# A decoder layer on one core: key masks as a GpSimd select, Silu in two rounds, the last batch in halves, new orders on every engine

## The chip, the core and the metric
One core of a Trainium2 chip runs the whole kernel as one program. Its engines are TensorE (PE, with the weight loads shown as PEld), VectorE (DVE), ScalarE (ACT), GpSimd (POOL) and SyncE (SP, which issues most DMAs). Each works through its own list in order; semaphores join them. The metric is the time of one execution in microseconds of the device.

## What is computed
One pre-norm decoder layer over x of (8, 128, 256), with softmax cut to what matters:

```python
x = x + attn(layernorm(x))     # 16 query heads, 4 key heads of width 16, rotary positions, causal
x = x + xattn(layernorm(x))    # scores = x @ ctx.T / 16, masked per batch, softmax, @ ctx
x = x + ffn(layernorm(x))
# attn: scores = einsum('bhgnd,bhsd->bhns', q, k) / 4, so a group's four query heads are summed;
#   then a causal softmax, @ v, @ Wo + bo
# ffn: x, w_gate_up, h and w_down each go through int8 and back, one scale per row
#   gate, up = split(xq @ w1q.T); h = silu(gate) * up; out = hq @ w2q.T     # inner width 704
```

## The kernel before
Everything is tiled by batch: 128 tokens are the 128 partitions, and there are eight batches, j = 0 to 7. Nothing loops at run time; `decoder_layer` writes one list of instructions per engine, and the list at the end of each engine's block (`keep_warm(30); mean_w_first(); ...`) is the order, written out by hand. Steps of different batches are interleaved in it, so that batch 5 may be in self attention while batch 3 is in cross attention. A step waits for the semaphores of its inputs (`done`), for a ring of two or three buffers (`free`), or for a PSUM bank that the batch before still occupies (`bank_free`, `bank_r_free`).

Start (loads and weights). DMAs: SP issues w_first (Wq, Wk, Wv), x_second, wo, x, xT, three parts of w1, ctxT, w2, ctx, in this order; ScalarE issues x_zero, x_first (x of batch 0 with the rotary table and the biases) and the mask. `keep_warm(n)` runs n products of zeros, bf16, 256 columns, that nothing uses. `mean_w_first` and `centre_w_first` take the mean off the projection weights. `bias_wo` (L271) builds the output weight with its bias, and VectorE sums and centres it (`sum_wo`, `mean_wo`, `centre_wo`, L744 to L752). VectorE also sums and rotates the biases (`sum_bias`, `rope_bias`, `rope_bias_sum`, L728 to L740). `mean_ctx` (L281) gives the mean over features of each context token: per batch and feature half one fp32 product with ctxT as weights and a single moving column.

Self attention of batch j. `project` (L295) gives q, k, v; VectorE's `rotate` (L781), GpSimd's `rotate_c` (L1007) and VectorE's `rotate_sum` (L791) apply the rotary table and the bias; `transpose_qk` (L303), ScalarE's `evacuate_qk` (L546). `mask_scores` (L314) writes the causal mask to PSUM by bf16 products of an identity with the mask, `scores` (L319) adds the scores, `max_scores` (L799) takes the row maximum, which is put into a spare row of q, transposed (`transpose_q_max`, L325) and copied (`evacuate_q_max`, L552). Then the scores are made again, transposed, keys on the partitions: `mask_other_keys` and `score_keys` write the transposed causal mask `causal_T` (L330) and add the products (L343). `exp_self` (L557) gives the probabilities p_self_T, `weigh_values` (L355, L358) their product with v and their sum, `invert_sums` (L804) and `normalise_y` (L808) the mean, `project_out` (L363) and `residual_1` (L814) x1.

Cross attention: `transpose_x1`, `cross_scores` (L379), `max_cross`, `bias_cross`, `exp_cross` (L573, Exp), `transpose_cross_p`, `readout` (L390), `residual_2` (L832). `centre_ctx` on GpSimd takes the mean off the context, from what mean_ctx gave.

FFN: x is quantised (`amax_x`, `quantise_x`) and transposed (`transpose_x_int`); `gate_product` (8 instructions of 352 columns) and `up_product` (4), both L447; `silu_gate` (L645, Silu, on both halves of 352 columns), `widen_gate` (L1029, GpSimd), `hidden` (L901), `amax_h` (L906), `scale_h`, `invert_h` (L915), `quantise_h` (L650), `transpose_h` (L474), `evacuate_h` (L638), `down` (L486), `scale_down` (L920), `add_residual` (L1056, the last on VectorE, L927), the store. All Exp calls come before the first Silu; ScalarE loads the tables of a function group by an instruction of its own. `transpose_gate`, `transpose_up`, `spread_up_scale` and `transpose_w2` bring the quantised weights into place between the batches.

## Time and profile before

| | us |
|---|---|
| median of three runs (111.39 to 113.15) | 111.41 |
| profiled execution, whole | 111.01 |
| its span, first to last instruction | 109.2 |
| PE busy | 96.1 |
| DVE, ACT, POOL busy | 75.5, 64.7, 60.2 |

The table's busy times are those of one profiled execution. Matmuls are pipelined, so a busy TensorE is not one at its peak: how many instructions start in a stretch, and at which granted clock, tells more. The time of a run is some 2 us longer than the span, for what lies around the instructions.

### The profile page before, as it was taken

Reading aid. Unit: us, or ns where it says so; the run is one execution under the profiler, and the core shown is the slowest. Engines: PE = TensorE matmul, PEld = TensorE weight load, DVE = VectorE, ACT = ScalarE, POOL = GpSimd, SP = SyncE. Lnnn points to the kernel's source line nnn. Section 1 sums busy time; section 2 is a strip of 40 time slices with the busy share of each in tenths; the row PEclk is TensorE's granted clock in tenths of the full one; section 3 lists DMA queues with packets and bytes.
Section 4 is the critical chain, followed back from the end, with each engine's and each line's share of the span. In section 5 each row is a group of like instructions: output and inputs, shape, how many; then the busy total and the mean of one; then the engine's idle time right before and its main releaser. Section 6 shows DMA issues by size and latency. Waiting matters only on the chain.

```text
span 109.2 us, 2451 instructions
## 1 busy us (share of the span) xinstructions
PE 96.1 (88%) x827; PEld 74.7 (68%) x827; DVE 75.5 (69%) x216; ACT 64.7 (59%) x169; POOL 60.2 (55%) x122
## 2 busy tenths in 40 slices
PE   6998396999999999999999998766799999999850
PEld 4786284799876677687688786445687888865520
DVE  5176939978669695956984846367698868889331
ACT  1300113870859748686668493889877587788620
POOL 6364402999358994135162143255888968765430
PEclk9999959985599999999999999999999999999999
DMA  2999999700000000000000000000000000111212
GB/s 53 382 331 405 417 420 388 230 0 0 0 9 0 0 0 3 6 0 0 0 6 0 0 0 0 9 0 0 0 0 0 0 0 6 51 48 48 96 54 96
DMA packets 4522, 8.35 MB, mean 76 GB/s; under 512 B 349, under 2 KB 3358, under 8 KB 4382
## 3 DMA queue, kind: packets, MB, share of 16 engines
q1 hardware_dynamic: 4206, 7.64, 19.2%
q10 hardware_dynamic: 304, 0.56, 1.4%
q8 instruction: 7, 0.11, 0.5%
q14 instruction: 5, 0.04, 0.1%
HBM read 7.15 MB, written 1.05 MB: 75 GB/s over the span
## 4 chain that ended last, share of the span: by engine, by line
PE 71%; DVE 12%; ACT 6%; DMA 4%; issue 3%; ACTq 1%; DVEq 0%
PE ps_s L447 15%; PE ps_q L295 7%; PE ps_r L281 5%; PE ps_y L486 5%; DMA mask_sb<-in_mask 4%; PE ps_s L343 3%; PE ps_y L363 3%; PE ps_r L390 3%; PE ps_s L319 3%; PE ps_x L379 3%; PE ps_x L474 3%; PE ps_q L303 2%; PE ps_y L355 2%; PE ps_s L330 2%; PE ps_s L314 2%
## 5 line engine op out<-in xcount | busy, mean ns | idle before, releaser
L1029 POOL TENSOR_TENSOR gate_up<-gate,up_row 128x704 f32<-128x704 f32 x8 | 13.6, 1700 | 3.0 <-ACT gate L645 2.9
L255 PE MATMUL ps_s<-warm 128*128 128x256 bf16 x51 | 9.4, 361 | 1.0 <-DVE warm L679 1.0
L1041 POOL TENSOR_SCALAR x_aug<-x2c 128x256 f32<-128x256 f32 x8 | 3.8, 480 | 10.5 <-DVE x2c L832 10.4
L540 ACT ACTIVATE v_pad<-ps_q,r 128x64 f32<-128x64 f32 x8 | 2.5, 314 | 11.9 <-DVE rot L781 11.9
L804 DVE RECIPROCAL y_rsum<-ps_y 128x128 f32<-128x128 f32 x8 | 7.6, 953 | 2.3 <-PE ps_y L358 2.1
L645 ACT ACTIVATE gate<-ps_s,x_scale 128x704 f32<-128x704 f32 x8 | 6.8, 847 | 3.9 <-PE ps_s L447 3.9
L901 DVE SCALAR_TENSOR_TENSOR hid<-ps_s,x_scale,gate_up 128x704 f32<-128x704 f32 x8 | 7.6, 949 | 1.7 <-PE ps_s L447 1.4
L255 PEld LDWEIGHTS ps_s<-warm 128*128 128x128 bf16 x51 | 6.5, 131 | 3.2 <-DVE warm L679 1.0
L447 PE MATMUL ps_s<-gate_hi,x_int_T 128*128 128x352 f32 x32 | 8.4, 343 | 0.0
L1007 POOL TENSOR_TENSOR rot_c<-rot,b_rope 128x128 f32<-128x128 f32 x8 | 3.6, 455 | 8.5 <-DVE rot L781 8.5
L486 PE MATMUL ps_y<-w_T,h_T 128*128 128x256 bf16 (+1 forms) x48 | 7.5, 276 | 0.6 <-DVE ffn L920 0.6
L447 PE MATMUL ps_s<-gate_lo,x_int_T 128*128 128x352 f32 x32 | 7.8, 323 | 0.0
L650 ACT ACTIVATE h_int<-hid,h_inv 128x704 int16<-128x704 f32 x8 | 7.0, 881 | 1.0 <-PE ps_x L474 0.8
L799 DVE TENSOR_REDUCE qk_rot<-ps_s 128x4 f32<-128x512 f32 x8 | 5.5, 690 | 2.7 <-PE ps_s L319 2.7
L1056 POOL TENSOR_TENSOR y_out<-ffn,x_aug 128x256 f32<-128x256 f32 x7 | 4.8, 690 | 4.4 <-DVE ffn L920 4.4
L781 DVE TENSOR_TENSOR rot<-ps_q,rope_r 128x256 f32<-128x256 f32 x8 | 3.4, 422 | 5.5 <-PE ps_q L295 5.3
L906 DVE TENSOR_REDUCE h_amax<-hid 128x1 f32<-128x704 f32 x8 | 7.0, 876 | 0.1
L920 DVE SCALAR_TENSOR_TENSOR ffn<-ps_y,h_scale,w_row 128x256 f32<-128x256 f32 x8 | 3.9, 482 | 4.5 <-PE ps_y L486 4.3
L447 PE MATMUL ps_s<-up_int,x_int_T 128*128 128x352 f32 x32 | 7.0, 339 | 0.0
L390 PE MATMUL ps_r<-ctx_aug,p_cross_T 128*128 128x257 f32 x16 | 5.2, 407 | 1.6 <-ACT x_int_T L631 0.7
L638 ACT CAST h_T<-ps_x 128x640 bf16<-128x640 int16 x8 | 5.5, 685 | 1.7 <-PE ps_x L474 1.7
L486 PEld LDWEIGHTS ps_y<-w_T,h_T 128*128 128x128 bf16 (+1 forms) x48 | 4.0, 97 | 3.4 <-issue 1.7
(165 smaller groups left out, 282.2 us busy)
## 6 DMA issues: line engine op xcount, KB each, us to landing
w_raw<-in_w SPq DMA_DIRECT2D x2, 512.0 KB, 9.5
ctxT<-in_ctxT SPq DMA_DIRECT2D x1, 1024.0 KB, 12.3
ctx_aug<-in_ctx SPq DMA_DIRECT2D x1, 1024.0 KB, 15.6
out_x<-y_out SPq DMA_DIRECT2D x8, 128.0 KB, 1.7
x_aug<-in_x SPq DMA_DIRECT2D x1, 768.0 KB, 7.4
xT<-in_xT SPq DMA_DIRECT2D x1, 768.0 KB, 8.6
w_raw<-in_w SPq DMA_DIRECT2D x1, 704.0 KB, 13.6
x_first<-in_x_first ACTq DMA_DIRECT2D x1, 416.0 KB, 5.6
```

Source lines behind the costliest of these rows:

```text
L255: nc.tensor.matmul(ps_s[:, H - 1, 0:2 * T], warm[:, 0:P], warm[:, :], start=True, stop=True)
L295: last = nc.tensor.matmul(ps_q[:, 0:6 * QK], x_feature(j, c), wqkv_c[:, c, :, :], start=c == 0, stop=c == DC - 1)
L390: nc.tensor.matmul(ps_r[:, 0:DA], p_cross_T[:, j, :], ctx_aug[:, j, :], start=True, stop=True).then_inc(s["readout_done"], 1)
L447: last = nc.tensor.matmul(ps_s[:, first + i, 0:FH], x_int_T[:, j, c, :], w[:, c, i * FH:(i + 1) * FH], start=c == 0 and w is parts[0], sto ...
L486: last = nc.tensor.matmul(ps_y[:, 0:D], h_T[j % 2][0:n, f, :], w2_T[0:n, f, :], start=f == 0, stop=f == FC - 1)
L638: nc.scalar.copy(h_T[j % 2][:, 0:FC - 1, :], src[:, 0:(FC - 1) * T].rearrange("p (f t) -> p f t", t=T))
L645: nc.scalar.activation(gate[j % 2][:, :, :], ps_s[:, 0:2, 0:FH], ACT.Silu, scale=x_scale[:, j:j + 1]).then_inc(s["gate_ready"], 1)
L650: nc.scalar.mul(h_int[j % 2][:, :], hid[j % 2][:, :, :].rearrange("p i f -> p (i f)"), h_inv[:, j:j + 1]).then_inc(s["h_int_ready"], 1)
L804: nc.vector.reciprocal(y_rsum[j % 3][:, :], ps_ys).then_inc(s["y_rsum_done"], 1)
L901: nc.vector.scalar_tensor_tensor(hid[j % 2][:, :, :], ps_s[:, 2:4, 0:FH], x_scale[:, j:j + 1], gate_up[j % 2][:, :, :], ALU.mult, ALU.mult ...
L906: nc.vector.tensor_reduce(h_amax[:, j:j + 1], hid[j % 2][:, :, :].rearrange("p i f -> p (i f)"), AX.X, ALU.max, apply_absolute_value=True) ...
L1029: nc.gpsimd.tensor_tensor(gate_up[j % 2][:, :, :], gate[j % 2][:, :, :], up_row[:, :].rearrange("p (i f) -> p i f", i=2), ALU.mult).then_i ...
```

## The change
- `causal_T` and its products go. `score_keys` starts its PSUM groups itself; after `exp_self`, GpSimd sets the probabilities of later keys to zero with a select over 128x512 (`drop_later_keys`), and `weigh_values` waits for that.
- `mean_ctx` has 60 moving columns per product instead of one, and results 61 columns apart; it stands ahead of `weigh_values(0)`. ctxT is loaded ahead of xT and w1; x_first moves to SP's queue, wo to ScalarE's.
- The bias sums and rotations move from VectorE to GpSimd (the key bias's copy to ScalarE), the centring of wo from VectorE to ScalarE.
- The warm products write to another bank and are spread differently (30, 6, 4, 11, 7, 2 for 30, 6, 10, 5).
- `silu_gate(0)` and `(1)` come before `exp_cross(6)` and `(7)`, the other Silu calls after them, so the tables change four times in place of two.
- `transpose_h` alternates between two banks. Batch 7's gate, Silu, widening (now on VectorE), hidden product, maximum, quantisation, transposes, copies and down product run in two halves.
- Every engine's list is written in a new order. Batches of the FFN start between the last attention batches.

Cut to its core; `last_transpose_h_a` and `_b`, `last_down_a` and `_b` `last_hidden`, `last_amax_h` and their like are the old steps on half the columns, and `sum_bias`, `rope_bias` and `centre_wo` the old arithmetic on another engine (five GpSimd operations for the bias):

```diff
             sp.dma_start(w_first[:, :], w_first_in).then_inc(s["w_first_loaded"], 16)
+            sp.dma_start(x_first[:, :], x_first_in).then_inc(s["x_first_loaded"], 16)
             sp.dma_start(x_second[:, :], x_second_in).then_inc(s["x_second_loaded"], 16)
-            sp.dma_start(wo_raw[:, :], wo_in).then_inc(s["wo_loaded"], 16)
             sp.dma_start(x_aug[:, 2:B, 0:D], x_in).then_inc(s["x_loaded"], 16)
+            sp.dma_start(ctxT[:, :, :, :], ctxT_in).then_inc(s["ctxT_loaded"], 16)
             sp.dma_start(xT[:, :, :, :], xT_in).then_inc(s["xT_loaded"], 16)
             for part, (first, last) in enumerate(W1_PARTS):
                 sp.dma_start(w1_raw[:, first:last, :], w1_in[:, first:last]).then_inc(s[f"w1_{part}_loaded"], 16)
-            sp.dma_start(ctxT[:, :, :, :], ctxT_in).then_inc(s["ctxT_loaded"], 16)
             sp.dma_start(w2_raw[:, :, :], w2_in).then_inc(s["w2_loaded"], 16)
...
-                    nc.tensor.matmul(ps_s[:, H - 1, 0:2 * T], warm[:, 0:P], warm[:, :], start=True, stop=True)
+                    nc.tensor.matmul(ps_r[:, 0:2 * T], warm[:, 0:P], warm[:, :], start=True, stop=True)
...
-                nc.tensor.matmul(ps_r[:, 0:B], mean_w[0:B, :], any_diag[:, :], start=True, stop=True)
+                means = ps_r[:, 0:B * CM].rearrange("p (b n) -> p b n", n=CM)
+                nc.tensor.matmul(means[:, :, 0], mean_w[0:B, :], any_diag[:, :], start=True, stop=True)
                 pe.wait_ge(s["ctxT_loaded"], 16)
                 for j in range(B):
                     for c in range(DC):
-                        last = nc.tensor.matmul(ps_r[:, B + j:B + j + 1], ctxT[:, j, c, :], mean_w[:, 0:1],
+                        last = nc.tensor.matmul(means[:, j, 1:CM], ctxT[:, j, c, :], mean_w[:, 1:CM],
                                                 start=c == 0, stop=c == DC - 1)
...
-            def mask_keys(j, heads):
-
-                for h in heads:
-                    nc.tensor.matmul(ps_s[:, h, 0:T], ident_b[:, :], causal_T[:, :], start=True, stop=False)
-
-            def mask_other_keys(j):
-                if j == 0:
-                    done(pe, "causal_T_ready", 0)
-                done(pe, "negmax_done", j)
-                mask_keys(j, range(1, H))
-
             def score_keys(j):
 
                 done(pe, "q_max_T_ready", j)
-                mask_keys(j, range(1))
                 for h in range(H):
                     nc.tensor.matmul(ps_s[:, h, 0:T], qk_T[j % 3][h * HP:(h + 1) * HP, 1, :],
-                                     q_max_T[j % 3][h * HP:(h + 1) * HP, :], start=False, stop=True).then_inc(s["keys_done"], 1)
+                                     q_max_T[j % 3][h * HP:(h + 1) * HP, :], start=True, stop=True).then_inc(s["keys_done"], 1)
...
-                done(pe, "p_T_ready", j)
+                done(pe, "p_causal_ready", j)
...
+            def last_gate(i):
+
+                if i == 0:
+                    gate_free(LAST)
+                    done(pe, "x_int_T_ready", LAST)
+                for c in range(DC):
+                    for w in (gate_hi, gate_lo):
+                        last = nc.tensor.matmul(ps_s[:, i, 0:FH], x_int_T[:, LAST, c, :], w[:, c, i * FH:(i + 1) * FH],
+                                                start=c == 0 and w is gate_hi, stop=c == DC - 1 and w is gate_lo)
+                last.then_inc(s["last_gate_done"], 1)
...
+                bank = (ps_x, ps_q)[j % 2]
...
-                bank_free(pe, "h_T_ready", j)
+                elif j == 1:
+                    done(pe, "qk_T_ready", B - 1)
+                free(pe, "h_T_ready", j, 2)
...
+            keep_warm(30); mean_w_first(); keep_warm(6); mask_scores(0); bias_wo(); keep_warm(4); project(0)
+            keep_warm(11); transpose_qk(0); scores(0); keep_warm(7); project(1); transpose_q_max(0)
+            keep_warm(2); score_keys(0); mean_ctx(None, 0); weigh_values(0); transpose_qk(1); mask_scores(1)
+            scores(1); project(2); project_out(0); transpose_q_max(1); transpose_gate(0, "valid_ready", 0)
+            score_keys(1); transpose_qk(2); transpose_x1(0); mask_scores(2); project(3); scores(2)
+            cross_scores(0); weigh_values(1); transpose_q_max(2); transpose_qk(3); score_keys(2)
+            transpose_gate(1, "gate_lo_ready", 0); project(4); mask_scores(3); project_out(1); scores(3)
+            transpose_cross_p(0); transpose_gate(2, "gate_lo_ready", 1); transpose_qk(4); weigh_values(2)
+            transpose_q_max(3); transpose_x1(1); project(5); score_keys(3); cross_scores(1); project_out(2)
+            readout(0, "gate_lo_ready", 2); mask_scores(4); transpose_qk(5); transpose_cross_p(1); scores(4)
+            transpose_x1(2); weigh_values(3); transpose_q_max(4); cross_scores(2); score_keys(4)
+            readout(1, "x2_ready", 0); project(6); mask_scores(5); project_out(3)
+            transpose_x_int(0, "x2_ready", 1); scores(5); transpose_cross_p(2); weigh_values(4)
+            readout(2, "x_int_T_ready", 0); transpose_q_max(5); transpose_x1(3); transpose_qk(6); score_keys(5)
+            cross_scores(3); project_out(4); mask_scores(6); project(7); scores(6); transpose_cross_p(3)
+            transpose_x_int(1, "x2_ready", 2); weigh_values(5); transpose_q_max(6); transpose_x1(4)
+            transpose_qk(7); score_keys(6); readout(3, "x_int_T_ready", 1); cross_scores(4); mask_scores(7)
+            spread_up_scale(0, "x2_ready", 3); scores(7); project_out(5); transpose_cross_p(4)
+            spread_up_scale(1, "up_row_ready", 0); transpose_q_max(7); transpose_x1(5); weigh_values(6)
+            readout(4, "up_row_ready", 1); score_keys(7); cross_scores(5); transpose_x_int(2, "x2_ready", 4)
+            gate_product(0); project_out(6); transpose_up(0, "x_int_T_ready", 2); transpose_cross_p(5)
+            weigh_values(7); gate_product(1); readout(5, "up_int_ready", 0); transpose_x1(6); project_out(7)
+            transpose_up(1, "x2_ready", 5); cross_scores(6); transpose_x_int(3, "up_int_ready", 1)
+            up_product(0); gate_product(2); transpose_x_int(4, "x_int_T_ready", 3); up_product(1)
+            transpose_cross_p(6); transpose_x_int(5, "x_int_T_ready", 4); transpose_x1(7)
+            readout(6, "x_int_T_ready", 5); cross_scores(7); transpose_w2(0, "x2_ready", 6); up_product(2)
+            transpose_cross_p(7); transpose_w2(1, "w2_ready", 0); gate_product(3); transpose_h(0)
+            readout(7, "w2_ready", 1); gate_product(4); transpose_h(1); up_product(3)
+            transpose_x_int(6, "x2_ready", 7); gate_product(5); down(0); up_product(4); gate_product(6)
+            up_product(5); transpose_h(2); down(1); transpose_x_int(7, "x_int_T_ready", 6); transpose_h(3)
+            up_product(6); last_gate(0); down(2); transpose_h(4); last_gate(1); down(3); up_product(7)
+            transpose_h(5); down(4); transpose_h(6); down(5); down(6); last_transpose_h_a()
+            last_transpose_h_b(); last_down_a(); last_down_b()
...
             act.dma_start(x_aug[:, 0, 0:D], x_zero_in).then_inc(s["x_zero_loaded"], 16)
-            act.dma_start(x_first[:, :], x_first_in).then_inc(s["x_first_loaded"], 16)
             act.dma_start(mask_sb[:, :], mask_in).then_inc(s["mask_loaded"], 16)
+            act.dma_start(wo_raw[:, :], wo_in).then_inc(s["wo_loaded"], 16)
...
+            copy_key_bias(); centre_wo(); scale_v(0); evacuate_qk(0); evacuate_q_max(0); scale_v(1); exp_self(0)
+            quantise_w1(0); quantise_w1(1); evacuate_qk(1); quantise_w1(2); quantise_w1(3); scale_v(2)
+            evacuate_q_max(1); square_1(0); upper_gate(0); exp_self(1); evacuate_qk(2); evacuate_x1(0)
+            quantise_w1(4); scale_v(3); quantise_w2(0); evacuate_q_max(2); evacuate_qk(3); exp_self(2)
+            upper_gate(1); exp_cross(0); quantise_w2(1); scale_v(4); evacuate_cross_p(0); upper_gate(2)
+            evacuate_qk(4); square_1(1); evacuate_q_max(3); evacuate_x1(1); scale_v(5); exp_self(3)
+            exp_cross(1); evacuate_cross_p(1); square_2(0); evacuate_x1(2); evacuate_q_max(4); square_1(2)
+            evacuate_qk(5); exp_self(4); quantise_x(0); square_2(1); exp_cross(2); evacuate_x_int(0); scale_v(6)
+            evacuate_cross_p(2); square_1(3); quantise_x(1); evacuate_q_max(5); evacuate_x1(3); evacuate_qk(6)
+            exp_self(5); square_2(2); exp_cross(3); quantise_x(2); scale_v(7); evacuate_cross_p(3); square_1(4)
+            evacuate_q_max(6); evacuate_x_int(1); evacuate_x1(4); exp_self(6); evacuate_qk(7); square_2(3)
+            exp_cross(4); evacuate_up_scale(0); evacuate_cross_p(4); evacuate_up_scale(1); evacuate_q_max(7)
+            square_1(5); evacuate_x1(5); quantise_x(3); exp_self(7); square_2(4); evacuate_x_int(2)
+            exp_cross(5); silu_gate(0); evacuate_up(0); evacuate_cross_p(5); quantise_x(4); square_1(6)
+            silu_gate(1); evacuate_x1(6); evacuate_up(1); quantise_x(5); evacuate_x_int(3); exp_cross(6)
+            evacuate_x_int(4); square_1(7); evacuate_cross_p(6); evacuate_x_int(5); evacuate_x1(7); square_2(5)
+            quantise_h(0); exp_cross(7); silu_gate(2); square_2(6); evacuate_cross_p(7); quantise_x(6)
+            silu_gate(3); quantise_h(1); evacuate_h(0); silu_gate(4); square_2(7); evacuate_x_int(6)
+            quantise_h(2); silu_gate(5); quantise_x(7); evacuate_h(1); quantise_h(3); silu_gate(6)
+            quantise_h(4); evacuate_x_int(7); evacuate_h(2); evacuate_h(3); last_silu(0); quantise_h(5)
+            last_silu(1); evacuate_h(4); quantise_h(6); evacuate_h(5); evacuate_h(6); last_quantise_h(0)
+            last_quantise_h(1); last_evacuate_h_a()
...
+            stats_1(0); aggregate_1(0, 1); sum_wq(); copy_ident(); find_valid(); centre_w_first(); stats_1(1)
+            aggregate_1(1, 2); exclude(); rotate(0); stats_1(2); rotate_sum(0); stats_1(3); stats_1(4)
+            stats_1(5); stats_1(6); max_scores(0); stats_1(7); aggregate_1(2, B); rotate(1)
+            amax_w1(0); scale_w1(0); invert_w1(0); rotate_sum(1); amax_w1(1); scale_w1(1); invert_w1(1)
+            invert_sums(0); keep_valid(); normalise_y(0); max_scores(1); rotate(2); residual_1(0); rotate_sum(2)
+            amax_w1(2); scale_w1(2); invert_w1(2); amax_w2(); scale_w2(); invert_w2(); rotate(3); max_scores(2)
+            rotate_sum(3); lower_gate(0); invert_sums(1); max_cross(0); normalise_y(1); bias_cross(0); rotate(4)
+            lower_gate(1); rotate_sum(4); residual_1(1); max_scores(3); invert_cross_sum(0); negate_ctx_mean()
+            invert_sums(2); normalise_y(2); rotate(5); lower_gate(2); max_cross(1); bias_cross(1); rotate_sum(5)
+            residual_2(0); residual_1(2); amax_x(0); max_scores(4); invert_cross_sum(1); invert_sums(3)
+            step_x(0); invert_x(0); normalise_y(3); max_cross(2); residual_2(1); bias_cross(2); amax_x(1)
+            rotate(6); residual_1(3); step_x(1); invert_x(1); max_scores(5); rotate_sum(6); invert_cross_sum(2)
+            invert_sums(4); residual_2(2); normalise_y(4); amax_x(2); max_cross(3); step_x(2); invert_x(2)
+            bias_cross(3); residual_1(4); rotate(7); max_scores(6); rotate_sum(7); invert_sums(5)
+            invert_cross_sum(3); normalise_y(5); residual_2(3); max_cross(4); bias_cross(4); amax_x(3)
+            max_scores(7); residual_1(5); invert_cross_sum(4); step_x(3); invert_x(3); residual_2(4)
+            invert_sums(6); max_cross(5); bias_cross(5); normalise_y(6); amax_x(4); step_x(4); invert_x(4)
+            invert_cross_sum(5); residual_1(6); invert_sums(7); normalise_y(7); residual_2(5); amax_x(5)
+            step_x(5); invert_x(5); residual_1(7); max_cross(6); bias_cross(6); hidden(0); amax_h(0)
+            scale_h(0); invert_h(0); invert_cross_sum(6); hidden(1); residual_2(6); max_cross(7); bias_cross(7)
+            amax_x(6); evacuate_w2(0); step_x(6); invert_x(6); amax_h(1); invert_cross_sum(7); evacuate_w2(1)
+            scale_h(1); invert_h(1); hidden(2); residual_2(7); amax_h(2); amax_x(7); scale_h(2); invert_h(2)
+            step_x(7); invert_x(7); hidden(3); amax_h(3); scale_h(3); invert_h(3); scale_down(0); hidden(4)
+            amax_h(4); scale_h(4); invert_h(4); hidden(5); scale_down(1); amax_h(5); hidden(6)
+            scale_h(5); invert_h(5); scale_down(2); amax_h(6); last_widen(0); scale_h(6); invert_h(6)
+            scale_down(3); last_hidden(0); last_widen(1); last_amax_h(0); scale_down(4); last_hidden(1)
+            last_amax_h(1); scale_down(5); last_scale_h(); scale_h(7); invert_h(7); scale_down(6)
+            last_evacuate_h_b(); scale_down(7); add_residual(7)
...
+            def drop_later_keys(j):
+
+                done(pool, "p_T_ready", j)
+                nc.gpsimd.affine_select(out=p_self_T[j % 3][:, :, :], in_=p_self_T[j % 3][:, :, :], compare_op=ALU.is_ge, fill=0.0, base=0,
+                                        pattern=[[0, H], [1, T]], channel_multiplier=-1).then_inc(s["p_causal_ready"], 1)
...
+            rstd_1(0, 1, 1); scale_rope(0); sum_bias(); rope_bias(); rotate_c(0); centre_x(0); rstd_1(1, 2, 2)
+            centre_x(1); scale_rope(1); rotate_c(1); rstd_1(2, B, 3); drop_later_keys(0); scale_rope(2)
+            centre_x(2); rescale_gate(0); scale_rope(3); rescale_gate(1); rotate_c(2); centre_x(3)
+            scale_rope(4); centre_x(4); rstd_2(0); drop_later_keys(1); rescale_gate(2); rotate_c(3); centre_x(5)
+            scale_rope(5); scale_rope(6); centre_x(6); centre_x(7); drop_later_keys(2); rotate_c(4)
+            scale_rope(7); centre_ctx(0); centre_ctx(1); rstd_2(1); rotate_c(5); drop_later_keys(3)
+            centre_ctx(2); whole_x2(0); rstd_2(2); scale_x(0); drop_later_keys(4); rotate_c(6); centre_ctx(3)
+            rstd_2(3); drop_later_keys(5); rotate_c(7); centre_ctx(4); scale_x(1); rstd_2(4); centre_ctx(5)
+            centre_ctx(6); drop_later_keys(6); centre_ctx(7); whole_x2(1); scale_x(2); rstd_2(5); scale_x(3)
+            drop_later_keys(7); whole_x2(2); widen_gate(0); scale_x(4); rstd_2(6); whole_x2(3); widen_gate(1)
+            rstd_2(7); scale_x(5); whole_x2(4); whole_x2(5); widen_gate(2); whole_x2(6); widen_gate(3)
+            scale_x(6); widen_gate(4); widen_gate(5); scale_x(7); widen_gate(6); add_residual(0); whole_x2(7)
+            add_residual(1); add_residual(2); add_residual(3); add_residual(4); add_residual(5); add_residual(6)
```

## Rows read from the trace of the kernel before
**Rows 1.** The page of before, parts 1 and 2: engines' busy time, granted clock.
```profile
PE 96.1 (88%) x827; PEld 74.7 (68%) x827; DVE 75.5 (69%) x216; ACT 64.7 (59%) x169; POOL 60.2 (55%) x122
...
PEclk9999959985599999999999999999999999999999
```

**Rows 2.** Windows: stretch, length, busy PE PEld DVE ACT POOL, PEclk, DMA.
```profile
0.00:31.35 31.35, 27.22 (x193) 22.24 (x193) 21.25 (x70) 9.65 (x23) 16.98 (x45) 0.84 0.62 229
31.35:60.00 28.65, 27.90 (x325) 21.48 (x322) 21.40 (x64) 21.44 (x71) 15.65 (x38) 1.00 0.01 2
60.00:80.00 20.00, 16.17 (x141) 12.37 (x137) 12.60 (x37) 14.87 (x44) 9.80 (x20) 1.00 0.01 1
80.00:98.00 18.00, 18.00 (x130) 14.70 (x129) 14.99 (x34) 13.73 (x23) 14.32 (x16) 1.00 0.05 16
98.00:109.20 11.20, 6.77 (x55) 3.93 (x52) 5.25 (x13) 4.98 (x11) 3.48 (x6) 0.99 0.21 72
```

**Rows 3.** Chain of waits: start us, us, engine, tile, line, instructions.
```profile
11.53 0.41 DVE rot L781
...
13.24 0.65 PE ps_q L303 x2
...
13.88 1.07 PE ps_s L255 x5
...
16.66 0.61 PE ps_s L319 x8
...
18.04 0.33 PE ps_s L325
...
18.96 0.43 PE ps_s L343 x8
...
21.70 5.19 PE ps_r L281 x32
...
28.80 1.58 PE ps_q L295 x4
...
35.98 0.65 PE ps_q L295 x4
```

**Rows 4.** Windows of line 281 alone (mean_ctx), columns as in rows 2.
```profile
22.50:23.00 0.50, 0.50 (x7) 0.50 (x6) 1.00 0.00 0
...
24.00:24.50 0.50, 0.50 (x4) 0.50 (x4) 0.50 0.00 0
```

**Rows 5.** The page, part 6: DMA issues, KB each, us to landing.
```profile
ctxT<-in_ctxT SPq DMA_DIRECT2D x1, 1024.0 KB, 12.3
...
xT<-in_xT SPq DMA_DIRECT2D x1, 768.0 KB, 8.6
```

**Rows 6.** Timeline of GpSimd: start, us, operation.
```profile
1.76 0.29 POOL L968 TENSOR_SCALAR_AFFINE_SELECT causal<-causal 128x128 bf16<-128x128 bf16 x1
...
12.09 0.45 POOL L1007 TENSOR_TENSOR rot_c<-rot,b_rope 128x128 f32<-128x128 f32 x1 [0.92 <-DVE rot L781]
...
19.17 1.34 POOL L987 TENSOR_TENSOR r<-ln_var,pow_exp 128x6 f32<-128x6 f32 x1
```

**Rows 7.** Chain of waits: a batch's key masks (L330), score masks (L314).
```profile
34.38 0.17 PE ps_s L330 x3
...
34.58 0.23 PE ps_s L330
...
37.58 0.22 PE ps_s L314 x4
```

**Rows 8.** Timeline of ScalarE: a copy of transposed q and k, the table load.
```profile
13.92 0.37 ACT L546 COPY qk_T<-ps_q 128x256 f32<-128x256 f32 x1 [1.56 <-PE ps_q L303]
...
73.02 1.28 ACT L645 ACT_TABLE_LOAD   x1
```

**Rows 9.** Chain of waits at the end: up_product(7), the last inverse.
```profile
97.19 0.84 PE ps_s L447 x4
...
100.97 0.17 DVE h_inv L915
```

245 lines of the change are left out of this document (113 added, 132 removed).

## Prediction
> **What bounds the kernel now.** I read the page's first two parts first. TensorE is busy 88% of the span, VectorE 69%, ScalarE 59%, GpSimd 55%, and the PEclk digits show two places where the clock fell, near slices 6 and 10 to 11 (2.73 us a slice) [rows 1]. Then the windows cut the span into five stretches [rows 2]. Up to 31.35 us TensorE is "busy" 27.22 us, but at a mean granted clock of 0.84. From 31.35 to 60 it is idle 28.65 - 27.90 = 0.75 us, from 60 to 80 idle 20.00 - 16.17 = 3.83 us, from 80 to 98 never, and in the last 11.2 us it is idle 4.4 us. So the span is TensorE's in-order queue, plus a poor start, a hole where attention's last batches hand over to the FFN, and a tail. The chain of waits, mostly TensorE lines, gives the places of the poor start [rows 3]: rotate(0) only at 11.53, scores(0) at 16.66, and one block of 5.19 us at 21.70, mean_ctx: 32 instructions with one moving column each. The windows on that line show what it is [rows 4]: 7 of them in half a microsecond at clock 1.00, then 4 in half a microsecond at 0.50. The clock falls inside this block (2.4 to 1.2 GHz) and stays down until after project(3), which takes 1.58 us where project(5) takes 0.65 [rows 3].
>
> **The start, step by step.** The comparison point is what the kernel has done at 31.35: score_keys(1), project(3), project_out(0) and transpose_gate(0).
> 1. Warm products 1 to 30 and mean_w_first are the same; the latter ends near 8.0. Behind it come 6 warm ones, 4 masks, bias_wo and 4 warm ones. A warm one costs 1.07/5 = 0.21 at the low clock [rows 3], so 0.11 at the full one, four masks 0.22 [rows 7], bias_wo as much as four warm ones: project(0) runs at about 9.8 to 10.6, 0.6 later than now. VectorE has lost the bias sums and the three wo steps, which now hold rotate(0) until 11.53; it starts near 10.65, 0.9 earlier. GpSimd now sums and ropes the bias, five operations of at most 0.45 us [rows 6] behind scale_rope(0), ready near 9.5 and so hidden; without that cover each late tenth would go into the transposes.
> 2. The transposes of batch 0 start at 12.35 instead of 13.24. Between them and scores(0) stand warm products, project(1) and the masks now; after, only ScalarE's copy (0.37) [rows 8]. The scores end at about 13.4, now at 16.66 + 0.61 = 17.27.
> 3. 7 warm ones (0.75), project(1) (0.65), the maximum's transpose (0.33), ScalarE's copy and score_keys (0.43) [rows 3] follow: about 15.9 instead of 19.39, **3.5 us earlier**. VectorE's maximum lies beside project(1).
> 4. mean_ctx comes next and needs ctxT, now issued ahead of xT and w1. ctxT lands 12.3 us after its issue now, xT 8.6 [rows 5], at about 11.4, when 2.8 MB are in; ctxT will have 0.25 MB more up to its end than xT has now, so it lands near 12, and xT near 14, both early enough. w1 slips by 1 MB, some 2.6 us, to about 15.4, just when VectorE's queue comes to it. The products have 60 moving columns instead of one. Fp32 streaming costs 0.65/4/192 = 0.85 ns a column and instruction [rows 3], so 60 columns take 0.05 us; a one-column instruction takes 0.5/7 = 0.071 [rows 4], its weight load. So the columns lie under the load: 32 x 0.071 = 2.3 us, if the clock holds. Bounds: 2.3 (holds) to 5.2 (falls as now). The fall now comes 1.9 us into nearly empty products; the new ones stream most of the time, and the dense stretch keeps 1.00 throughout [rows 2]. I take 2.3: **-2.9 us**.
> 5. The rest to the comparison point takes 2.3 (19.39 to 21.70) + 4.5 (26.89 to 31.35) = 6.8 us now, 3.5 us of it at half clock. After: 1.75 less for the clock, 0.6 less for two batches without masks, 0.6 more because weigh_values(0) must wait for GpSimd, whose queue runs rotate_c(1) and rstd_1(2, B) (1.34 for the power alone [rows 6]) ahead of the first select. So 5.0: **-1.8 us**.
> Together 3.5 + 2.9 + 1.8 = **8.2 us**; the point is reached at about 23.2.
>
> **31.35 to 98.** This stretch has 62.07 us of TensorE work and 4.58 idle [rows 2].
> - Key masks gone: four bf16 products per batch. From below the row of mask_scores' four, 0.22; from above 0.17 + 0.23 = 0.40 [rows 7]. I take 0.3, between, for six batches: **-1.8 us** (1.3 to 2.4).
> - The select on GpSimd, 128x512, is not in the trace. The nearest row is the same operation on 128 columns, 0.29 [rows 6]; so from 0.29 to 4 x 0.29 = 1.16. I take 0.85, nearer the full multiple, 7 us in all. GpSimd is busy 15.65 of 28.65 us in the dense stretch [rows 2], so it fits. But the select sits in an in-order queue between exp_self and weigh_values, behind rotate_c, rstd_2 and centre_ctx. TensorE's order has projections, a transpose of the next maximum or cross scores in between, so I cost the latency at nothing. Where that cover is gone it is a select plus one queued operation, some 1.4 us a batch.
> - VectorE and ScalarE come under pressure. TensorE reaches the dense part 8 us earlier, VectorE with about 4 us of its weight work still to do (it has done 21.25 by 31.35 now). Laying its queue out beside TensorE's from 23.2, I have about 36 us of VectorE work for the attention batches beside 40 of TensorE; max_scores(2) would end near 27.0 while TensorE is there at 25.6. I count some 4 us of such stalls down to max_scores(7), mostly at the maximum's transpose and at project_out.
> - The hole of 3.83 us goes in exchange: three gate_products and two up_products now lie between the last cross batches, and VectorE's and ScalarE's chains of cross 5, 6 and 7 run beside them. The price is two more table loads of 1.28 us on ScalarE [rows 8], one before exp_cross(6), one before silu_gate(2). ScalarE is busy 14.87 of 20 us there [rows 2]: 2.6 more fit, with 2.5 over. Queued behind each load are the probabilities' copy or a gate's copy, for which TensorE waits; the products cover that. The row shows the load itself.
>   The Trainium skill (ScalarE: Activation LUTs, What ACT_TABLE_LOAD costs) gives about 2.66 us for each switch with its drain, and its rules advise grouping calls by table set, which speaks against this edit; by its price the two would be 5.3 us. No wait of that kind stands in the rows here.
> - So 4 to 5 us of stalls take the place of 4.58 idle: net **0** (-2, if the other engines keep up, to +3).
>
> **The tail.** From the end of up_product(7), 98.0, to the end it is 11.2 us now, and the last inverse is ready 3.1 after it [rows 9]. After, half a widen and one more scale_down stand in VectorE's queue before it, each some 0.5 by the 0.41 of a 256-column operation [rows 3]: +4.1. But the first half is quantised, transposed and used while the second follows, and down(6) is done before: TensorE ends at +6.8 instead of +8.0, the span at +10. That is 1.2 less, but transpose_h(4) and down(3), some 1.3 us, have moved ahead of that point. Net **0** (-1 to +1).
>
> **Sum.** 109.2 - 8.2 - 1.8 = 99.2 us of span. The profiled execution took 111.0 as a whole, 1.8 over its span, the median of three runs 111.4, 2.2 over it. 99.2 + 2.2 = 101.4; forecast **101.5 us**. Bounds: masks +-0.5, stalls -2 to +3, tail +-1, mean_ctx +2.9.
>
> **Rivals.**
> - A, the clock falls in or behind mean_ctx all the same. For it: it falls here now, and once before, after TensorE had waited for batch 0's transposes [rows 1]; the new start still has short waits. Against: 60 columns stream. 2.9 plus up to 1.75 back: 103.5 to 106. Chance 0.17.
> - B, VectorE and ScalarE become the bound of the attention part. Over 31.35 to 98 they are busy 49.0 and 50.0 of 66.65 us now [rows 2], would reach some 84%, and over 90% before the gates, and each hop costs a semaphore. Stalls of 7 to 10 rather than 4.6: 104 to 107. Chance 0.15.
> - C, the hole closes without new stalls, because the new orders give each wait cover: 97 to 99.5. Chance 0.10.
> - D, the other side: the select decides. In its in-order queue each weigh_values waits for one select and what stands before it. 1.3 us a batch beyond the cover, over eight batches, give back all 10 us: 111 or more. It decides only if the select takes about 2 us, which no row suggests. Chance 0.03.
> - E, the two switches find no cover and the chain of cross 6 and 7 is as long as now: 3.8 us of hole stay, and 2.6 for the loads: about 107.5. Chance 0.05.
> - The forecast: 0.50, its own range 99.5 to 103.5.
>
> The range reaches into A and B above and C below: 98.5 to 105.5, with 2 in 10 left out. About 2% is what a measurement of this kernel can tell from no change. Faster: all but D and the far ends of B and E, 0.94; same 0.03; slower 0.03.
>
> **What the profile would show.** Right: no low PEclk digit in slices 7 to 12; mean_ctx 2.2 to 2.6 us; rotate(0) near 10.7; score_keys(0) ending near 15.9; the comparison point near 23 to 24; the first gate_product near 56 to 58 (now 63.6); TensorE idle 4 to 5 us before up_product(7), spread over waits for the maximum and y_T; four table loads of 1.28. Wrong: a low clock beside mean_ctx (A); VectorE over 90% busy from 25 to 55 with TensorE idle more than 6 (B); the select over 1.2 us with waits for it at the head of TensorE's list (D).

## The result, and the profile after

| | before | after |
|---|---|---|
| median, us (range) | 111.40 (111.09 to 113.15) | 103.96 (103.75 to 104.16) |
| profiled execution, us | 111.01 | 103.75 |
| its span, us | 109.2 | 102.0 |
| ratio after/before, 95% interval | | 0.9355 (0.9312 to 0.9398) |

The kernel became 7.4 us faster by this comparison; 9.9 was forecast. The profiled span is 7.2 us shorter. On other chips the kernel before took 108.9 to 110.1 us at a mean granted clock near 0.96 and 110.6 to 111.3 near 0.95, and the executions here are like the latter or longer, so that like against like, on the chip where after was timed again, the gain is 5.8 us (109.56 against 103.78, ratio 0.9443, 0.9372 to 0.9513).

The page of after, parts 1 and 2 (as [rows 1]): the engines' busy time, and the granted clock in 40 slices of 2.55 us.

```profile
PE 91.4 (90%) x804; PEld 69.4 (68%) x804; DVE 74.9 (73%) x215; ACT 68.0 (67%) x177; POOL 65.0 (64%) x132
...
PEclk9999999999999999999999999999999999999955
```

TensorE has 4.7 us less busy time and 2.5 us less idle time (10.6 for 13.1). The low digits near slices 6 and 10 are gone. Two new ones stand at the very end.

The windows of after, cut where the same work is done as at the cuts of [rows 2] (columns: stretch, its length, busy time and count of PE, PEld, DVE, ACT, POOL, granted clock, DMA share, GB/s).

```profile
0.00:24.20 24.20, 21.43 (x188) 17.56 (x188) 15.93 (x55) 9.95 (x27) 15.91 (x42) 1.00 0.81 296
24.20:56.90 32.70, 31.45 (x345) 23.09 (x343) 27.49 (x78) 24.39 (x80) 23.07 (x53) 1.00 0.01 2
56.90:76.20 19.30, 17.28 (x128) 13.62 (x129) 13.26 (x41) 16.83 (x40) 12.05 (x22) 1.00 0.01 1
76.20:91.34 15.14, 15.14 (x107) 11.99 (x108) 12.65 (x29) 13.04 (x26) 11.33 (x15) 1.00 0.08 28
91.34:102.00 10.66, 6.06 (x42) 3.15 (x39) 5.58 (x15) 3.78 (x8) 2.60 (x4) 0.77 0.18 62
```

That gives the account. Up to the comparison point 24.2 us where it was 31.35: -7.2. From there to the end of up_product(7) 67.1 us where it was 98.03 - 31.35 = 66.7: +0.5. The tail 10.66 where it was 11.2: -0.5. Together 109.2 - 7.2 + 0.5 - 0.5 = 102.0. The gain is in the start, as forecast, but 1.0 smaller than its term. The middle was forecast at -0.5 (1.8 less for the key masks, 1.3 more for work moved in ahead of its end) and the tail at 10.0.

Not all of the start's 7.2 us is the change's. TensorE's first 30 warm products are the same in every kernel but for the bank they write, yet they took between 4.8 and 6.1 us in the profiled executions. TensorE's timeline of before, and then that of after:

```profile
1.04 6.09 PE L255 MATMUL ps_s<-warm 128*128 128x256 bf16 x30 [1.04 <-DVE warm L679]
...
7.81 0.82 PE L255 MATMUL ps_s<-warm 128*128 128x256 bf16 x6
...
21.63 5.26 PE L281 MATMUL ps_r<-mean_w,ctxT 128*128 128x1 f32 x32
```

```profile
1.10 5.33 PE L259 MATMUL ps_r<-warm 128*128 128x256 bf16 x30 [1.10 <-DVE warm L761]
...
7.12 0.82 PE L259 MATMUL ps_r<-warm 128*128 128x256 bf16 x6
```

The second group of warm products starts at 7.81 and at 7.12, so 0.7 us of the difference was there before the two lists part. Counted from that group, the start is 23.5 us before and 17.1 after: -6.5, not -7.2. Further, before's low clock near slice 6 is not in every execution: the kernel before with 60 columns (below) has the same list up to mean_ctx, has no low clock ahead of it, and starts it at 20.29 instead of 21.63 (1.2 us earlier, counted from the second group). None of the twelve profiles with the new start has that early fall.

The chain of waits in the start, which answers [rows 3] (start us, us, engine, tile, line, instructions), and under it TensorE's timeline of the same kernel for the steps that the chain does not pass through.

```profile
9.85 0.44 DVE rot L836
...
11.53 0.45 PE ps_q L308 x2
...
12.43 0.62 PE ps_s L324 x8
```

```profile
14.92 0.50 PE L336 MATMUL ps_s<-q_max_T,qk_T 32*128 32x128 f32 x8
...
15.46 3.78 PE L286 MATMUL ps_r<-mean_w,ctxT 128*128 128x60 f32 x32
19.17 0.43 PE L348 MATMUL ps_y<-p_self_T,v_pad 128*32 128x128 f32 x8
```

rotate(0) is at 9.85 instead of 11.53, scores(0) end at 13.05 instead of 17.27, score_keys(0) at 15.4 instead of 19.39. mean_ctx takes 3.78 us instead of 5.26 (5.19 in the chain of [rows 3]), all at full clock.

The longest waits of TensorE (what waited, for whom, us in total, times, longest).

```profile
PE ps_s L440 <- ACT gate L713: 1.2, 2, 0.7
...
PE ps_q L308 <- DVE qk_rot L846: 1.0, 3, 0.6
PE ps_s L324 <- ACT qk_T L595: 0.7, 2, 0.5
PE ps_y L520 <- DVE ffn L1007: 0.7, 1, 0.7
PE ps_s L330 <- DVE qk_rot L854: 0.6, 1, 0.6
```

The longest in the middle is new: gate products that wait for a Silu whose table is being loaded. The timelines show it, first ScalarE's, then TensorE's product that was held up (the bracket is the idle time ahead of it, and who ended it).

```profile
58.57 1.28 ACT L713 ACT_TABLE_LOAD   x1 [0.42 <-PE ps_s L440]
59.87 0.85 ACT L713 ACTIVATE gate<-ps_s,x_scale 128x704 f32<-128x704 f32 x1
...
65.52 1.28 ACT L622 ACT_TABLE_LOAD   x1
...
71.31 1.28 ACT L713 ACT_TABLE_LOAD   x1
```

```profile
60.77 0.59 PE L440 MATMUL ps_s<-gate_hi,x_int_T 128*128 128x352 f32 x2 [0.68 <-ACT gate L713]
...
73.50 0.59 PE L440 MATMUL ps_s<-gate_hi,x_int_T 128*128 128x352 f32 x2 [0.52 <-ACT gate L713]
```

The load does not start while ScalarE idles for the gate product (0.42 us); it starts when that wait is over, so 1.28 + 0.85 us lie between the product and its Silu's end.

The select, on GpSimd: the page's group (its mean of one is 639 ns) and, from the timeline, the first of the eight.

```profile
L1111 POOL TENSOR_SCALAR_AFFINE_SELECT p_self_T<-p_self_T 128x512 f32<-128x512 f32 x8 | 5.1, 639 | 1.5 <-ACT p_self_T L606 1.4
```

```profile
17.39 0.64 POOL L1111 TENSOR_SCALAR_AFFINE_SELECT p_self_T<-p_self_T 128x512 f32<-128x512 f32 x1
```

It takes 0.64 us, and no wait of TensorE for it is in the list.

### The profile page after: what moved, and what is told of

Read it like the earlier page. It is cut to its first block, busy times and chain, and to the rows that moved or that the text cites. A ratio compares the mean times of both kernels' runs of the same rounds, so it can differ in the third digit from the quotient of the medians.

```text
span 102.0 us, 2428 instructions
## 1 busy us (share of the span) xinstructions
PE 91.4 (90%) x804; PEld 69.4 (68%) x804; DVE 74.9 (73%) x215; ACT 68.0 (67%) x177; POOL 65.0 (64%) x132
## 4 chain that ended last, share of the span: by engine, by line
PE 58%; DVE 14%; ACT 11%; POOL 8%; issue 6%; DVEq 0%; ACTq 0%; POOLq 0%
PE ps_s L440 13%; PE ps_r L259 6%; PE ps_r L383 4%; PE ps_y L520 3%; PE ps_s L324 3%; PE ps_q L300 3%; ACT L713 3%; PE ps_y L356 2%; PE ps_s L336 2%; PE ps_q L308 2%; DVE qk_rot L846 2%; POOL rot_c L1106 2%; PE ps_y L348 2%; POOL w_q L1125 2%; ACT gate L713 2%
## 5 line engine op out<-in xcount | busy, mean ns | idle before, releaser
L1134 POOL TENSOR_TENSOR gate_up<-gate,up_row 128x704 f32<-128x704 f32 x7 | 11.9, 1704 | 4.9 <-ACT gate L713 4.9
L259 PE MATMUL ps_r<-warm 128*128 128x256 bf16 x60 | 9.4, 318 | 1.1 <-DVE warm L761 1.1
L988 DVE SCALAR_TENSOR_TENSOR hid<-ps_s,x_scale,gate_up 128x704 f32<-128x704 f32 x7 | 6.6, 948 | 3.4 <-PE ps_s L440 2.1
L259 PEld LDWEIGHTS ps_r<-warm 128*128 128x128 bf16 x60 | 6.7, 115 | 2.9 <-DVE warm L761 1.1
L440 PE MATMUL ps_s<-gate_hi,x_int_T 128*128 128x352 f32 x28 | 7.3, 342 | 1.3 <-ACT gate L713 1.2
L713 ACT ACTIVATE gate<-ps_s,x_scale 128x704 f32<-128x704 f32 x7 | 5.9, 847 | 1.5 <-PE ps_s L440 1.4
L887 DVE SCALAR_TENSOR_TENSOR x2c<-ps_r,c_rsum,x1c 128x257 f32<-128x257 f32 x8 | 3.8, 470 | 4.1 <-PE ps_r L383 4.1
L440 PEld LDWEIGHTS ps_s<-gate_hi,x_int_T 128*128 128x128 f32 x28 | 4.6, 188 | 2.2 <-ACT gate L713 2.0
L1111 POOL TENSOR_SCALAR_AFFINE_SELECT p_self_T<-p_self_T 128x512 f32<-128x512 f32 x8 | 5.1, 639 | 1.5 <-ACT p_self_T L606 1.4
L606 ACT ACTIVATE p_self_T<-ps_s 128x512 f32<-128x512 f32 x8 | 4.8, 597 | 1.5 <-PE ps_s L336 1.4
L595 ACT COPY qk_T<-ps_q 128x256 f32<-128x256 f32 x8 | 3.0, 375 | 3.8 <-PE ps_q L308 3.8
```

The lines of the kernel that those rows point to most:

```text
L259: nc.tensor.matmul(ps_r[:, 0:2 * T], warm[:, 0:P], warm[:, :], start=True, stop=True)
L440: last = nc.tensor.matmul(ps_s[:, first + i, 0:FH], x_int_T[:, j, c, :], w[:, c, i * FH:(i + 1) * FH], start=c == 0 and w is parts[0], sto ...
L713: nc.scalar.activation(gate[j % 2][:, :, :], ps_s[:, 0:2, 0:FH], ACT.Silu, scale=x_scale[:, j:j + 1]).then_inc(s["gate_ready"], 1)
L988: nc.vector.scalar_tensor_tensor(hid[j % 2][:, :, :], ps_s[:, 2:4, 0:FH], scale, gate_up[j % 2][:, :, :], ALU.mult, ALU.mult).then_inc(s[" ...
L1111: nc.gpsimd.affine_select(out=p_self_T[j % 3][:, :, :], in_=p_self_T[j % 3][:, :, :], compare_op=ALU.is_ge, fill=0.0, base=0, pattern=[[0, ...
L1134: nc.gpsimd.tensor_tensor(gate_up[j % 2][:, :, :], gate[j % 2][:, :, :], up_row[:, :].rearrange("p (i f) -> p i f", i=2), ALU.mult).then_i ...
```

## The experiments

Each was timed beside the kernel before on the same chip. The median of before moved between chips (109.7, 109.9, 110.6, and 111.4 above), that of after hardly did (103.96 and 103.78). So between calls I compare medians and spans of the changed kernels, and take the ratio only against before.

My theory: the start gains because the clock no longer falls, and because batch 0 has fewer things ahead of it; the middle gains nothing because small waits, and the Silu behind its table load, take the place of the hole. The rivals: the clock is not what the 60 columns buy; the select, or the lost mask products, decide; the halves decide.

Since the first 30 warm products take a different time in each execution, spans are compared from the start of the second group of warm products. From there the kernel after repeats to a few hundredths of a microsecond up to its tail. In us, from the profiles, to the start of each step named:

| kernel | to the first gate_product | to up_product(7) | to the end |
|---|---|---|---|
| before | 55.8 | 89.3 | 101.4 |
| after | 49.8 | 83.3 | 94.9 |
| after once more | 49.8 | 83.3 | 94.4 |
| one moving column | 51.8 | 85.4 | 96.4 |
| thirty columns | 51.3 | 84.8 | 95.8 |
| no table switch | 49.8 | 81.8 | 92.9 |
| first table early | 49.8 | 83.0 | 94.1 |
| Silu in one round | 49.8 | 90.3 | 101.9 |
| tanh | 50.5 | 87.2 | 98.8 |
| key masks back | 50.6 | 84.1 | 95.2 |
| no key masking | 49.5 | 83.0 | 94.1 |
| last batch whole | 49.8 | 83.3 | 95.9 |
| warm products in the tail | 49.8 | 83.3 | 94.4 |

The clock was low at the last products of after, of one round, of tanh and of the whole last batch, which costs after 0.5 us against its repetition; the last column is to be read with that.

**One moving column in the kernel after.** Does the clock fall again?

```diff
-  nc.tensor.matmul(means[:, j, 1:CM], ctxT[:, j, c, :], mean_w[:, 1:CM],
+  nc.tensor.matmul(means[:, j, 1:1 + 1], ctxT[:, j, c, :], mean_w[:, 1:1 + 1],
```

> The changed kernel with one moving column per mean_ctx product again instead of 60 (places of the results, order and everything else as changed). Theory (the nearly empty columns make the clock fall): the block of 32 starts at 0.07 us an instruction, the granted clock falls to 0.50 inside or right behind it as before the change, the block takes 3.5 to 5.2 us and what follows runs at half clock for up to 3.4 us; the whole is 1 to 3 us slower than the changed kernel, 105 to 107 us. Rival (the filled start alone, with its new warm products, holds the clock): the block takes 32 x 0.071 = 2.3 us instead of 3.8, the clock stays at 1.00, and the kernel is up to 1.5 us faster, 102.5 to 104 us.

Measured: 105.64 us (105.34 to 105.96), ratio 0.9615 (0.9544 to 0.9686), span 103.6. Its granted clock by slices, its block, and windows of the block's first part, its end and what follows:

```profile
PEclk9999999655999999999999999999999999999999
```

```profile
15.50 4.05 PE L286 MATMUL ps_r<-mean_w,ctxT 128*128 128x1 f32 x32
```

```profile
14.50:17.30 2.80, 2.66 (x30) 2.36 (x28) 2.73 (x9) 1.87 (x5) 2.01 (x4) 1.00 1.03 409
17.30:20.70 3.40, 3.40 (x35) 2.97 (x35) 0.95 (x3) 1.01 (x3) 3.40 (x8) 0.71 1.05 365
20.70:24.10 3.40, 3.37 (x19) 2.81 (x19) 1.98 (x4) 1.97 (x5) 0.59 (x2) 0.50 0.10 33
```

The clock falls inside the block, near its end, and stays at the lower level (1.2 GHz) to 25.5. One column buys no time: 4.05 us against 3.78 with 60. By the table 2.0 us are lost up to the first gate product, 0.3 of them in the block, the rest behind it. The theory holds for the clock; its pace in the block, 0.07 us an instruction, does not.

**Thirty columns.** The same edit with `1 + 30`.

> The changed kernel with 30 moving columns in mean_ctx instead of 60. The block of 32 took 3.78 us with 60 columns, 0.118 us an instruction, while one column took 0.071. If weight load and stream add up (0.071 + 0.8 ns a column): 0.095 us, 3.0 us for the block, and 0.7 us less in all if the clock holds. If the columns lie under the load, as the prediction had it: 3.8 us again, because something else costs those 0.047. Whether 30 columns hold the clock: theory, yes (1.00 through the block and behind it); rival, it falls as with one column and the kernel is 1 to 2 us slower.

Measured: 105.48 us (105.47 to 105.49), ratio 0.9627 (0.9587 to 0.9666), span 103.7.

```profile
PEclk9999999855799999999999999999999999999996
```

```profile
16.21 3.76 PE L286 MATMUL ps_r<-mean_w,ctxT 128*128 128x30 f32 x32
```

The block holds the clock to its end and the clock falls right behind it: project(2) takes 1.65 us, 0.92 in the kernel after. 30 columns take 3.76 us, as good as the 3.78 of 60, and don't keep the clock: the rival held. It is no accident of one execution: the mean granted clock was 0.959 or 0.960 in all four, and 0.976 to 1.000 in the eight of after. So 3.76 / 32 = 0.117 us is the time of an instruction, whatever it streams up to 60 columns.

**Sixty columns in the kernel before.** This one part alone, with the place of mean_ctx as it was.

```diff
-  nc.tensor.matmul(ps_r[:, B + j:B + j + 1], ctxT[:, j, c, :], mean_w[:, 0:1],
+  nc.tensor.matmul(means[:, j, 1:CM], ctxT[:, j, c, :], mean_w[:, 1:CM],
```

> The kernel before with 60 moving columns in mean_ctx (and the results read from their new places), nothing else. Theory: the clock stays at 1.00 through the block, which takes 3.8 us instead of 5.2, and the 3.4 us behind it run at full clock: 1.4 + 1.7 = 3.1 us less, 108 to 109 us. Rival (the earlier idle stretch or the low fill of the old start makes the clock fall here all the same): 111 us or more, block 5 us or longer.

Measured: 107.59 us (106.62 to 108.3), ratio 0.9716 (0.9613 to 0.982): 2 to 3 us on that chip. Its block:

```profile
20.29 3.78 PE L283 MATMUL ps_r<-mean_w,ctxT 128*128 128x60 f32 x32
```

The block is 3.78 us at full clock, where before has 5.26. From the block's end to the masks of the next batch it takes 2.98 us where it took 4.40 (23.91 to 26.89, and 26.75 to 31.15). So the columns alone bring 1.5 us in the block and 1.4 behind it, with the block in its old place. (The clock fell once in this profile too, to 0.5 in one late slice, in the old hole; two of the four executions, at a mean clock of 0.992, took 106.6 and 106.9 us.)

**No table switch between the rounds.** Exp stands where Silu stood in all batches, so that ScalarE never changes tables; the FFN's values are other ones.

```diff
-  ... ps_s[:, 0:2, 0:FH], ACT.Silu, scale=x_scale[:, j:j + 1])
+  ... ps_s[:, 0:2, 0:FH], ACT.Exp, scale=x_scale[:, j:j + 1])
```

> The changed kernel with Exp computed where Silu is, so that ScalarE never changes tables (the FFN's values are not those of the layer); order and sizes unchanged. It takes 3 x 1.28 us off ScalarE, each in the stretch from 57 to 76. Theory (TensorE's waits for the gate's copy at 60.1 and 73.0, 0.7 + 0.5 us, and those around exp_cross(6), stand behind the loads): 1.0 to 2.0 us less, 102 to 103 us. Rival (the loads are covered and the stretch is held by VectorE's chain): within 0.3 us of the changed kernel.

Measured: 101.47 us (101.26 to 102.26), ratio 0.9249 (0.9173 to 0.9324), span 99.5. The window that answers the third of after:

```profile
56.90:76.20 19.30, 18.52 (x141) 14.81 (x141) 14.89 (x45) 14.19 (x38) 13.65 (x22) 1.00 0.00 1
```

The waits for gate L713 are gone, 13 more of TensorE's instructions lie in the stretch, and up_product(7) ends at 89.35 instead of 91.34. But 0.5 of that is the first warm products, which took 4.79 us here: the first gate product, ahead of any of the switches, is already at 56.46 instead of 56.93. By the table the three loads cost 1.5 us. The medians differ by 2.3 to 2.5, of which each kernel's own scatter is 1.0 or so. All of the 1.5 stands at the two loads ahead of a Silu (0.7 us each time); the one ahead of exp_cross(6) is covered. I had the two added ones at nothing.

**The first Silu table loaded early.** One dummy Silu on one element, which waits for nothing.

```diff
-            exp_cross(5); silu_gate(0); evacuate_up(0); ...
+            exp_cross(5); load_silu(); silu_gate(0); evacuate_up(0); ...
```

> The changed kernel with a one-element Silu behind exp_cross(5), which makes ScalarE load the Silu table before it waits for gate_product(0); now it waits 0.42 us for that product and loads then. Theory (gate_product(1) waits 0.7 us for that gate's copy): the load starts 0.4 us earlier, gate_product(1) too, 0.2 to 0.4 us less in all, 103.4 to 103.6. Rival (the gain is lost at the next wait, exp_cross(6)'s load at 65.5, which stands behind up_int's copy): no difference.

Measured: 103.25 us (103.24 to 103.71), ratio 0.9357 (0.9273 to 0.9441), span 101.5. The load now starts 0.02 us behind the operation ahead of it, without the 0.42 us of idle time; TensorE's waits for the gate fall from 1.2 to 0.9 us in total:

```profile
60.75 0.59 PE L441 MATMUL ps_s<-gate_hi,x_int_T 128*128 128x352 f32 x2 [0.37 <-ACT gate L717]
```

By the table that is the whole gain, 0.3 us, and it lasts to the end; the span is 0.5 shorter because the clock stayed up in this tail and not in that of after. This is the fastest kernel of the case that computes the layer, though the 0.5 to 0.7 us by which its median beats after come from different chips and are near their scatter.

**Silu in one round.** All Silu calls after the last cross softmax, with two loads instead of four; the FFN batches between move behind it on every engine. The order is mine, written by hand.

```diff
-            weigh_values(7); gate_product(1); readout(5, "up_int_ready", 0); ...
-            ... transpose_w2(0, "x2_ready", 6); up_product(2)
+            weigh_values(7); readout(5, "up_int_ready", 0); ...
+            transpose_cross_p(7); transpose_w2(1, "w2_ready", 0); gate_product(1); readout(7, ...)
+            up_product(1); gate_product(2); up_product(2); gate_product(3); ...
```

> The changed kernel with all Silu calls behind exp_cross(7) again: gate_product(1), (2), up_product(1), (2), hidden(0), (1) and their widenings moved behind the last cross scores on every engine, two table loads fewer on ScalarE. Theory (the two rounds close the hole in which TensorE waits for the chains of cross 6 and 7): 1 to 3 us slower, 105 to 107 us, with waits at transpose_cross_p, readout and gate_product(1). Rival (the two extra loads, 2.6 us of ScalarE, cost as much as the second round brings): 103.3 to 104.3, no difference.

Measured: 111.28 us (110.02 to 112.66), ratio 1.0084 (1.0045 to 1.0123), span 109.1. The window again, and the head of the list of TensorE's waits:

```profile
56.90:76.20 19.30, 13.38 (x99) 9.62 (x98) 10.63 (x36) 12.61 (x36) 9.98 (x19) 1.00 0.00 1
```

```profile
PE ps_r L383 <- DVE w_row L949: 3.4, 1, 3.4
```

The hole is back: 5.9 us idle instead of 2.0, and right behind it the clock falls:

```profile
76.20:80.00 3.80, 3.80 (x17) 3.77 (x16) 3.23 (x8) 0.45 (x2) 0.00 (x0) 0.59 0.00 0
```

All of the gain over before is lost, 7.0 us by the table. But 3.4 us of it is one wait of my own order, from 72.4 to 75.8: readout(7) waits for the second copy of w2, which I had put on VectorE behind hidden(0) and its maximum. The low clock comes straight after that wait and may hang on it; it lasts some 3.3 us of a busy TensorE, at half speed up to 1.7 us lost, by estimate. So 7.0 - 3.4 - 1.7 = 1.9 us are left to the two rounds if all of that is my order's fault, and 7 by the run as it stands. For this order the rounds are worth more than their loads; a better order in one round was not tried.

**Tanh for the first three gates.** Silu(x) written as x/2 (1 + tanh(x/2)), where the product by 1 + tanh goes to VectorE, so that no load stands between the softmaxes if tanh shares exp's table.

```diff
+  nc.scalar.activation(gate[j % 2][:, :, :], ps_s[:, 0:2, 0:FH], ACT.Tanh, scale=x_half[:, j:j + 1])
+  nc.vector.scalar_tensor_tensor(gate[j % 2][:, :, :], gate[j % 2][:, :, :], 1.0, ps_s[:, 0:2, 0:FH],
+                                 ALU.add, ALU.mult)
```

> The changed kernel with silu(g) of batches 0, 1 and 2 as g/2 (1 + tanh(g/2)): tanh on ScalarE, then one VectorE product with the gate's PSUM (3 x 0.95 us more on VectorE), two small GpSimd operations each. If tanh shares the table of exp, ScalarE loads twice instead of four times, the second load before Silu of batch 3, where it waits 0.8 us now. Without any switch the kernel took 2.0 us less. Theory: VectorE has idle stretches of 0.8 and 1.3 us at the first two places, so 0.7 to 1.5 us of the 2.0 are kept: 102.3 to 103.1. Rival (PSUM is held until VectorE's product, and VectorE is the next bound): 103.5 or more. If tanh has a table of its own, there are more loads and it is 1 to 3 us slower.

Measured: 107.94 us (107.68 to 108.38), ratio 0.9772 (0.966 to 0.9883), span 106.4. Only two loads are left, the second at 78.24, so the table is shared. But the head of TensorE's waits is now

```profile
PE ps_r L425 <- DVE w_row L957: 1.9, 1, 1.9
PE ps_s L442 <- ACT gate L722: 1.3, 1, 1.3
PE ps_r L405 <- DVE x2c L896: 1.2, 1, 1.2
...
PE ps_y L350 <- POOL p_self_T L1128: 1.0, 2, 0.7
```

VectorE is busy 77.4 us instead of 74.9, and its three new operations, in the middle of its queue, put two waits of 1.9 and 1.2 us on TensorE; the 1.3 is the second load, behind its wait as before. The last line is new too: weigh_values now waits for the select, 1.0 us in all, behind the two small operations (0.26 us each) that each of these gates adds to GpSimd's queue; by the table 0.7 us are lost before the first gate product. The kernel is 4 us slower than after. The rival held, with GpSimd's queue as a part of it.

**The key masks back, the select gone.**

```diff
+            def mask_keys(j, heads):
+                for h in heads:
+                    nc.tensor.matmul(ps_s[:, h, 0:T], ident_b[:, :], causal_T[:, :], start=True, stop=False)
-  ... q_max_T[j % 3][h * HP:(h + 1) * HP, :], start=True, stop=True)
+  ... q_max_T[j % 3][h * HP:(h + 1) * HP, :], start=False, stop=True)
```

> The changed kernel with the select on GpSimd undone: the 32 key mask products back on TensorE, right behind the transpose of the maximum as before, weigh_values waits for exp_self alone. By the prediction's term: 8 x 0.3 = 2.4 us more work on TensorE, less up to 0.5 us of waiting for the select: 105.5 to 106.5 us. Rival (the products only fill time in which TensorE waited for ScalarE's copy of the maximum, and the select's latency costs as much as they do): 103.5 to 104.5 us, no difference.

Measured: 104.55 us (103.68 to 105.62), ratio 0.946 (0.9356 to 0.9565), span 102.7. That is 0.6 to 0.7 us over after, by medians of different chips whose ranges overlap. From TensorE's timeline, a batch's four mask products in their two places:

```profile
34.10 0.33 PE L336 MATMUL ps_s<-causal_T,ident_b 128*128 128x128 bf16 x3
34.27 0.39 PE L375 MATMUL ps_x<-ident,x1c 128*128 128x128 f32 x2
...
35.15 0.22 PE L336 MATMUL ps_s<-causal_T,ident_b 128*128 128x128 bf16 x1
35.30 0.50 PE L349 MATMUL ps_s<-q_max_T,qk_T 32*128 32x128 f32 x8
```

The next work starts 0.17 us after the three and 0.15 after the one, so a batch's masks are 0.3 us, as I had them, and TensorE is busy 92.9 - 91.4 = 1.5 us longer. But the span is only 0.7 longer, and 0.8 by the table, all of it ahead of the first gate product: the rest went into waits that were there anyway.

**No key masking at all.** Neither masks nor select, so later keys are not left out; this prices the select.

> The changed kernel without any causal masking of the second scores: no select on GpSimd and no mask products on TensorE (the self attention's probabilities of later keys stay in). What is saved against the changed kernel is the whole price of the select: 8 x 0.64 us of GpSimd and its latency before weigh_values. Theory (covered except at batch 0 and 7, whose weigh_values follow closely): 0 to 0.7 us less, 103.3 to 104. Rival (each weigh_values waits for it, or GpSimd's list is the bound of 25 to 55 us): 2 us or more less, 102 or below.

Measured: 103.42 us (103.24 to 103.61), ratio 0.9439 (0.9398 to 0.9479), span 101.6. The kernel after on the same chip took 103.78. So eight selects of 0.64 us, 5.1 us of GpSimd's time, cost at most 0.4 us; by the table 0.3. The table also gives the masks alone, from this kernel to the one with the masks back: 50.6 - 49.5 = 1.1 us.

**The last batch whole.** Batch 7's gate, hidden product, quantisation and down product as in the other batches.

```diff
-            transpose_h(5); down(4); transpose_h(6); down(5); down(6); last_transpose_h_a()
-            last_transpose_h_b(); last_down_a(); last_down_b()
+            transpose_h(5); down(4); transpose_h(6); down(5); transpose_h(7); down(6); down(7)
```

> The changed kernel with batch 7 of the FFN in one piece again (one gate_product, Silu, widening on GpSimd, hidden, maximum, quantisation, transposes, copies, down product), everything before it as changed. The prediction's tail had the halves 1.2 us shorter from the end of up_product(7) to the end: then this is 104.8 to 105.3 us, against 103.8 for the changed kernel. Rival (VectorE's extra halves and the wait for the last scale_downs eat the gain): 103.5 to 104.3.

Measured: 104.34 us (103.46 to 104.87), ratio 0.9437 (0.9333 to 0.9541), span 102.5. Its waits list has

```profile
PE ps_q L487 <- ACT h_int L723: 1.3, 1, 1.3
```

where after has 0.4 for its half. The tail is 11.7 instead of 10.7. That up_product(7) ends 0.5 earlier is only that the first warm products took 4.83 us here; by the table it is where it was. So the halves are worth 1.0 us in these two profiles. Both have a low clock at the end, and here more of the last products fall into it (the last down product takes 1.57 us instead of 0.93, the one before it 1.24), which I estimate at 0.9 us against the 0.5 of after; with the clock up some 0.5 to 0.6 would be left. The medians give 0.4 to 0.6. That is between 0.5 and 1.0, less than the 1.2 I had given them.

**The kernel after once more, and warm products in its tail.** The second has 13 extra products between the last down products.

```diff
-            ... down(5); down(6); last_transpose_h_a()
-            last_transpose_h_b(); last_down_a(); last_down_b()
+            ... down(5); keep_warm_last(6); down(6)
+            keep_warm_last(4); last_transpose_h_a(); last_transpose_h_b(); keep_warm_last(3); last_down_a(); last_down_b()
```

> The changed kernel as it is, as the measure for the runs beside it on this chip. Theory: its time within 1 us of the first measurement (103.96); in some executions the clock falls in the last 5 us, in some not, and that is worth some 0.8 us (the last down product took 0.80 + 0.76 us at the low clock, 0.4 + 0.5 at the full one).

> The changed kernel with 6, 4 and 3 warm products in TensorE's waits behind up_product(7): before down(6), before the last transposes and before the last down product. Theory (the clock falls there because TensorE waits for VectorE and ScalarE): the granted clock stays 1.00 to the end, the last down product's two halves take 0.4 + 0.5 us, 0 to 0.8 us less than the changed kernel, and its runs scatter less. Rival (the fall depends on where the chip's window lies, or the warm products delay the chain): within 0.2 us or slower.

Measured: 103.78 us (102.81 to 103.82) for the same kernel, 103.95 (103.04 to 104.25) with the warm products. The last down products in the profile of after, and in that of its repetition:

```profile
97.24 0.80 PE L529 MATMUL ps_y<-w_T,h_T 128*128 128x256 bf16 x3
```

```profile
97.82 0.49 PE L529 MATMUL ps_y<-w_T,h_T 128*128 128x256 bf16 x3
```

In one execution the clock falls just ahead of them (0.54 in the window from 97 to 99), in the next it doesn't; there the first warm products ended 0.6 later, and the spans are 102.0 and 102.1. By the table the fall costs 0.5 us. The extra products did keep the clock up (a mean of 0.994 to 1.000 in all four executions; four of the eight of after have 0.976 to 0.978), and their kernel ends at 94.4 like the repetition. But the medians show no gain.

## Why the prediction was right or wrong

The time lies 2.5 us above the forecast and inside its range. The way and the place of the gain were right, its size was put too high: 9.9 us, where 7.4 were measured, and 5.8 like against like. Mean_ctx, the key masks, the table loads and the halves were each priced in the change's favour, and less idle time in the middle gave a part back.

**The clock.** Right. No low digit in slices 7 to 12; the one-column and the 30-column kernel bring it back, and 60 columns alone take it away in the kernel before. Rival A did not come.

**The start, steps 1 to 3 (-3.5).** Right, 4.0 us earlier for score_keys(0), but with luck: rotate(0) came at 9.85, not 10.65, because project(0) ran at 9.09 and not at 9.8, and that is the 0.7 us by which the first warm products happened to be faster in the profile of after. Without it 3.3 us, 0.2 less than forecast. And the forecast took over the early clock fall of the profile of before, which another execution of the same list did not have; it is 1.2 us of the 3.3.

**mean_ctx, step 4 (-2.9).** Wrong by 1.5 us, a mis-sized term: 3.78 us, not 2.3. I took "(x7)" in half a microsecond [rows 4] as seven instructions started. It counts those that overlap the stretch, and each of them lies in the records for 275 ns, so it takes in the ones begun before. In 1.6 us of the block in after it counts 16, where 1.6 / 0.117 = 13.7 start. The block of before fits the right figure: the clock fell 1.9 us into it, which is 16 instructions at 0.117, and the other 16 took 0.206 each in the 3.3 us left, somewhat under twice as long. The mechanism, columns hidden under the weight load, held: 1, 30 and 60 columns take the same.

**The rest to the comparison point, step 5 (-1.8).** Measured 24.2 - 15.4 - 3.8 = 5.0 us: as forecast. weigh_values(0) did not wait for the select, which was through at 18.03, before the longer mean_ctx ended at 19.2. So the start's sum was 8.2 forecast, 7.2 measured, 6.5 without the luck of the first warm products.

**Key masks (-1.8).** Each batch's price on TensorE was right (0.3), but not all of it reached the end: with the 0.6 of step 5 the forecast had 2.4 us for eight batches, the masks alone are worth 1.1, and 0.8 in exchange for the select. I took the stretch as bound by TensorE because it was 97% busy. A busy record can hide a short wait: the three mask products' record lasts 0.33 us while the next work starts after 0.17, so an idle gap of some 0.2 us between such products does not show. That the chain there passes through VectorE and GpSimd in such gaps is my explanation; no run isolates them.

**The select at nothing.** Right: 0.64 us in place of 0.85, and 0.3 us in all, at most 0.4. Rival D did not come.

**VectorE.** Right in kind. TensorE's wait of 0.6 us for a maximum is that of batch 2: in VectorE's queue the weights' maxima (0.95 and 1.59 us, from 23.60 to 26.48) stand ahead of it, and the maximum ends at 27.9, where I had 27.0. From 24.2 to 56.9 VectorE is busy 27.5 of 32.7 us, 84%; rival B did not come in this kernel; in the one with tanh VectorE's queue, and GpSimd's, did hold TensorE up.

**The hole and the loads (net 0).** The first gate_product is at 56.93, as forecast. Idle time is 2.0 us between 56.9 and 76.2 where it was 3.83 from 60 to 80, and 3.3 in the whole middle, less than the 4 to 5 forecast. In the one-round kernel the idle time is back, which speaks for the two rounds as the cause, with the reserve on its order. So rival C did not come (97 to 99.5 us), and of rival E the loads came in part and the hole did not. The failed step is "the products cover that": two of the three loads stand between a gate product and its Silu, with the next gate product queued behind it, and TensorE waits 0.7 and 0.5 us. The kernel without switches shows 1.5 us for all three, 0.7 at each of these two and nothing at the third.

The Trainium skill (ScalarE: Activation LUTs, What ACT_TABLE_LOAD costs) gives about 2.66 us for a switch with its drain. By the page the two added ones were to cost 5.3 us; all three together cost 1.5 of the kernel's time (2.3 to 2.5 by the medians), the load is 1.28 us, and the next ACTIVATE starts 0.02 us behind it. The measurement decides: no drain stands between the two in these traces. Its advice to group calls by table set was followed by the one-round kernel, which lost by it, in the order written for it: what the second round fills is a hole of TensorE's.

**The tail (0).** The inverse came at +4.0 (forecast +4.1), the span's end at +10.66 instead of +10, of which 0.5 is the clock at the last six products. The halves' 1.2 was mis-sized: 0.5 to 1.0.

**The sum.** By stretches: the start 24.2 for 23.2, the middle 67.1 for 66.2 (66.7 - 1.8 + 1.3), the tail 10.7 for 10.0; together 2.6 of the 2.8 us between 99.2 and 102.0, the rest is rounding. The start's +1.0 is mean_ctx's +1.5 and 0.2 ahead of it, less the 0.7 of the first warm products; the middle's +0.9 is masks that gave too little and loads that were not covered, less idle time that went. The time around the span was 1.8 in the profiled execution and 2.0 by the median, where the forecast took 2.2.

**Open.** How the middle's +0.5 divides between masks that freed time, loads that took it, and VectorE's queue: the single prices (masks and select -0.8, loads +1.5 for all three, the second round -1.9 to -7) don't fix it, because each was measured with the others in place. Whether the new start keeps the early clock fall away, or it comes and goes by execution there too, is not settled. And how much of the one-round kernel's loss is its hand-made order.

## What to carry to other kernels

A count in a window of overlapping instructions is not a rate: take the distance between starts, or the group's time over its count. Where the clock falls in or behind a block of products that stream next to nothing behind a large weight load, try giving them columns: here up to 60 cost no time. Two spans differ by what happened before the lists part: the first 30 warm products moved them by up to 1.3 us, more than most of the effects looked for, and counting from an instruction behind them took that out. A table load is worth paying where it fills a hole of the busiest engine with another stage's work; then look at what stands between the load and the wait it sits behind, and pull the load ahead of that wait with a dummy call.

## What the runs showed of the hardware

- The same 30 warm products at the start (bf16, 256 columns) took 4.79 to 6.09 us, from one profiled execution to the next.
- An fp32 weight load of 128 columns with its matmul took 0.117 us from start to start at the full clock, with 1, 30 or 60 moving columns (blocks of 32: 4.05 us with the clock falling inside, 3.76 and 3.78).
- With 30 moving columns the granted clock fell to the lower level behind the block, with 60 it stayed at 1.00, though TensorE is 100% busy by the records in both.
- A select on GpSimd over 128x512 fp32 took 0.64 us, little over twice that of 128x128 in bf16 (0.29).
- A table load does not start while ScalarE waits for its ACTIVATE's semaphore; with a dummy call ahead it started 0.02 us behind the operation before it, not 0.42. Tanh and Exp share a table (no load between them in the kernel with tanh).
